# Layer 0 of a two-layer kernel: each product with C directly behind its scan on VectorE

## What is computed

```python
x = hs @ in_proj_w.T                                  # 768 -> 1536 channels
xs = conv3x3_depthwise(x) + conv_b;  xs = xs * sigmoid(xs)
x_dbl = xs_seq @ x_proj_w.T
dt, Bs, Cs = split(x_dbl, [R, R + 4])
delta = softplus(dt @ dt_w.T + dt_b)
dA  = exp(delta[..., None] * A)                       # 4 states per channel
dBu = (delta * u)[..., None] * Bs
states = scan over the pixels:  s = dA * s + dBu
y = einsum('bdln,bln->bdl', states, Cs) + D_param * u
y = layernorm(y over channels);  out = y @ out_proj_w.T
x = x + out
```

## Time and profile before

| | |
|---|---|
| median of 3 runs | 3685.06 us (3684.29 to 3686.72) |
| the profiled execution, its own time | 3683.9 us |
| its span in the profile | 3682.1 us |
| mean granted TensorE clock | 0.967 |
| end of layer 0 in the profile | about 2772 us |
| the slots with scans (17 to 208) | from 263 to about 2715 us |
| page: busy, TensorE / VectorE / ScalarE / GpSimd | 92% / 78% / 64% / 64% of the span |

### The profile page before, as it was taken

One profiled execution on the slowest core, in us unless ns is written; L12 is line 12 of the kernel. 1 busy time (PEld: TensorE's weight loads), 2 busy tenths in 40 slices (PEclk: granted clock), 3 DMA queues, 4 the chain that ended last, 5 costly groups with the idle time before them and its releaser, 6 DMA issues. The chain is left out here.

```text
span 3682.1 us, 39373 instructions
## 1 busy us (share of the span) xinstructions
PE 3382.5 (92%) x10888; PEld 1745.1 (47%) x10888; DVE 2868.8 (78%) x4117; ACT 2345.9 (64%) x4095; POOL 2346.0 (64%) x1557
## 2 busy tenths in 40 slices
PE   5875799999999999999999999998798999999999
PEld 4432234333343344334333343343346877767787
DVE  4469999999999988999999999998754345565532
ACT  1357787887878867877788777887535555443211
POOL 0139898999989978898998989999830001112211
PEclk7897799999999999999999999999899999999999
DMA  7244355555556545555555555555533223356654
GB/s 288 81 144 118 92 137 150 153 148 147 139 149 159 145 130 131 149 142 146 158 144 150 134 147 160 136 160 146 139 87 114 66 83 107 117 191 210 209 199 153
DMA packets 217179, 529.93 MB, mean 144 GB/s; under 512 B 24744, under 2 KB 45928, under 8 KB 214016
## 3 DMA queue, kind: packets, MB, share of 16 engines
q1 hardware_dynamic: 173952, 376.39, 32.5%
q0 software_dynamic: 43008, 151.02, 18.5%
HBM read 346.17 MB, written 80.48 MB: 116 GB/s over the span
## 5 line engine op out<-in xcount | busy, mean ns | idle before, releaser
L575 PE MATMUL p_in<-xn,win_v 128*128 128x512 f32 (+1 forms) x2304 | 1064.3, 611 | 125.4 <-ACT halo L766 83.0
L591 PE MATMUL p_op<-uy,wout_ring 128*128 128x512 f32 x2160 | 987.5, 606 | 39.0 <-DVE x_res L970 38.9
L935 DVE TENSOR_TENSOR_SCAN p_da<-p_da,state,g_ring 128x512 f32<-128x512 f32 x672 | 827.3, 1277 | 107.9 <-ACT p_da L725 70.3
L907 POOL TENSOR_TENSOR g_ring<-du,B_bc 128x2048 f32<-128x2048 f32 x192 | 870.7, 4535 | 16.7 <-DMA B_bc<-bc_scratch 1.8
L956 DVE SCALAR_TENSOR_TENSOR p_cv<-win_v,conv_w,p_cv 128x512 f32<-128x512 f32 x960 | 722.8, 753 | 87.9 <-ACT p_cv L787 67.0
L575 PEld LDWEIGHTS p_in<-xn,win_v 128*128 128x128 f32 x2304 | 440.8, 197 | 705.8 <-issue 705.8
L591 PEld LDWEIGHTS p_op<-uy,wout_ring 128*128 128x128 f32 x2160 | 401.1, 192 | 614.2 <-issue 539.9
L725 ACT ACTIVATE p_da<-delta,A 128x512 f32<-128x512 f32 x768 | 499.4, 682 | 12.5 <-ACT state L730 0.2
L941 DVE TENSOR_TENSOR g_ring<-p_da,C_bc 128x512 f32<-128x512 f32 x768 | 486.9, 675 | 0.0
L1387 PE MATMUL banks<-x_split,w_split 128*128 128x512 f32 x1152 | 458.9, 398 | 11.0 <-DVE x_split L1590 5.5
L1389 PE MATMUL banks<-x_split,w_split 128*128 128x512 f32 x1152 | 450.4, 391 | 0.0
(11 more groups left out here) (220 smaller groups left out, 4070.3 us busy)
## 6 DMA issues: line engine op xcount, KB each, us to landing
g_ring<-g_ring POOLq DMA_DIRECT2D x192, 512.0 KB, 5.6
win_v<-in_win SPq DMA_DIRECT2D x192, 384.0 KB, 3.1
wout_ring<-wout_scratch SPq DMA_DIRECT2D x184, 384.0 KB, 3.8
x_ring<-x_scratch SPq DMA_DIRECT2D x192, 256.0 KB, 2.7
q_scratch<-q_ring POOLq DMA_DIRECT2D x96, 256.0 KB, 2.5
x_split<-q_scratch SPq DMA_DIRECT2D x96, 256.0 KB, 3.4
out<-x_ring POOLq DMA_DIRECT2D x96, 256.0 KB, 3.0
x_res<-in_x SPq DMA_DIRECT2D x90, 256.0 KB, 4.5
```

The source lines that it names most:

```text
L575: last = nc.tensor.matmul(p_in[:, 0:n], WR[:, i % NW, t, :], XN[:, t, off:off + n], start=(t == 0), stop=(t == XT - 1))
L591: last = nc.tensor.matmul(p_op[:], OR[:, e % NO, k - h * HALF, :], ucol(c * K + k), start=(k == 0), stop=(k == K - 1))
L907: nc.gpsimd.tensor_tensor(G[:, i % NG], DU[:].unsqueeze(1).broadcast_to([P, NS, N]), BB[:], ALU.mult).then_inc(s_dbu, 1)
L935: nc.vector.tensor_tensor_scan(bank, bank, G[:, i % NG, n, :], init, ALU.mult, ALU.add)\
```

## The change

In both places of VectorE's list where two scans were followed by two products, each product now stands directly behind its scan. Nothing is added or taken away, no wait is changed, and the lists of the other four engines are the same.

```diff
                     if a is not None:
                         scan(a, 0)
+                        times_c(a, 0)
                         scan(a, 1)
-                        times_c(a, 0)
                         times_c(a, 1)
...
                     if a is not None:
                         scan(a, 2)
+                        times_c(a, 2)
                         scan(a, 3)
-                        times_c(a, 2)
                         times_c(a, 3)
```

## The result

| | before | changed |
|---|---|---|
| median | 3684.68 us (3682.61 to 3686.72, 4 runs) | 3767.12 us (3763.60 to 3770.37, 4 runs) |
| ratio | | 1.0223, 95% interval 1.0210 to 1.0235: slower by 82.4 us |
| profiled execution, its span | 3683.9, 3682.1 us | 3770.37, 3768.6 us |
| mean granted TensorE clock | 0.967 | 0.960 |

The sign and the range of the prediction held; the number, 3739, was 28 us too low. The profiled execution after is 3.3 us above its median, so between the two profiled spans there are 86.5 us to explain.

A forecast was written before the change was run, and what follows sets the result against it. In a regular chunk VectorE sets the pace for 8.5 slots and TensorE for 3.5. Terms +3.4, +20.0, 0, +20.7 and +9.6 sum to +54 us on 3683.9, 3738; with 1.2 for the median, 3739, range 3712 to 3783.

The forecast's parts named there:

- The link: VectorE product directly behind its own scan: 0.09 overlap lost plus 0.035 hole, 0.127 us each, 98 us in all.
- Rival 1: The scan-to-product link is free, the drain being there anyway: nothing added, 3685 us; chance 5%.
- 8.5 slots: Slot 64 to first pair of slot 72, where VectorE sets the pace: 4.3 us more per regular chunk.
- waits at 67 and 72: VectorE's short waits for ScalarE's exponentials before these slots, swallowing about 0.6, leaving 3.7 us a chunk.
- 11.4 regular chunks: Twelve-slot chunks at 3.7 us: 5.4 from 463 to 1290 us (+20.0), six from 1508.7 to 2428.6 (+20.7).
- waits of 2.14 and 2.01: VectorE's waits before scan 2 of slot 63 and scan 0 of slot 64: still there, but smaller.
- Behind the last taps: Closed loop of VectorE and ScalarE, 4.91 us a pair instead of 4.66; its stretch, 2428.6 to 2679.8 us, +9.6.
- Slots 17 to 32: 250 to 463 us: 7.6 us more VectorE work against 4.9 us of waits for exponentials, +3.4 us.
- The cover: In a chunk's other 3.5 slots, the 2.14 us wait before slot 63's scan 2 covers the added 1.8 us.
- Rival 3: Nothing is covered, all 98 us of added VectorE time show: 3783 us; chance 13%.
- Rival 2: Only the one-way path counts, slots 64, 65, 68, 69: 2.0 us a chunk, +32 us, 3717; chance 14%.
- 1290 to 1508.7 us: Around the second image's start: VectorE stood 24.3 us in 13 waits, TensorE 95% busy, so 0 added.

The follow-up runs named there:

- e1_phase_tail: Scan and product alternate only in slots with S % 12 = 1, 2, 3, against the kernel before: 3691.79 us, ratio 1.0018.
- e2_phase_body: Scan and product alternate only in slots from S % 12 = 4 on, against the kernel before: 3757.18 us, ratio 1.0188.
- e11_middle_only: Scan and product alternate only in slots 97 to 111, against the kernel before: one run, 3692.18 us.
- e7_spaced_alternate: The changed kernel's alternation with a tap put between each scan and its product: 3813.30 us, ratio 1.0345 against the kernel before.

## Why the prediction was right or wrong

- **The link.** "Hole of 0.035, overlap of 0.09 lost": right to the nanosecond the trace can show (34 to 36 ns in 538 links). The term that was mis-sized is 0.127 a link, 0.51 a slot: it is 0.15 and 0.60. What was missing is the length: a product behind its own scan takes 692 ns instead of 675, and the second scan of a pair, no longer behind the first, 1283 instead of 1268. I had read the mean of the taps, 753, which mixes 743 and 756; their spread before the change would have shown that a dependent instruction is longer. A link here is always both, one instruction reads what its neighbour wrote and waits for its semaphore; no run parts the two. By 192 slots this is 115 us of VectorE's time instead of 98, and the page's busy time agrees: 86.9 us more, with 768 holes of 0.035 (27 us) that do not count as busy.
- **The rule of the Trainium skill** (VectorE: DVE Perf Modes, "The DRAIN you can't avoid"), that the pipeline empties anyway and a semaphore between two operations costs nothing extra, is not what these runs show: independent neighbours start 0.08 to 0.09 us before the other's end, dependent ones 0.035 behind it and are longer. The prediction took only half of that section of the Trainium skill: it also says that a next operation that is not held starts earlier, and with that the overlap of independent neighbours agrees. Rival 1 falls by all 538 links.
- **What reaches the end.** The count of 8.5 slots was right: 8.5 x 0.60 = 5.1, less 0.3 for the wait before slot 67 and 0.1 at slot 72, gives 4.7; 4.6 was measured at full clock. The prediction let the waits at 67 and 72 swallow 0.6, they gave 0.4: the one at 67 shrank to 0.07 instead of going. Over the 11.4 regular chunks the mis-sized link and these waits are 0.9 x 11.4 = 10 us of the 28 that were missing. The waits of 2.14 and 2.01 are smaller and not gone, as said. Behind the last taps 4.95 a pair came where 4.91 was predicted, and the stretch gave 10.5 for 9.6; it also has 10.3 us more at half clock, so that part of this agreement may be luck. Slots 17 to 32 gave 5.3 for 3.4: 15 slots at 0.09 more are 1.4 of that difference.
- **The cover** in slots 61 to 63 holds: `e1_phase_tail` left the chunk at 153.7. Rival 3 (3783, nothing covered) falls, although the time came out closer to it than to the forecast: it was nearly right by number and wrong by mechanism. Rival 2 (2 us a chunk) falls by `e2_phase_body`.
- **1290 to 1508.7 us, "0".** Right for VectorE's time (`e11_middle_only`), wrong for the sum: +7.2 us. The step that failed was that TensorE's own speed would stay as it was. The prediction had no term for the clock, although its own rows show one stretch at 0.93. In slots 32 to 112 of the changed kernel the clock stood at half for 34 us where the kernel before had no fall; 5.4 chunks at 4.6 explain 25 of the 31.0 us of slots 32 to 97, the rest and the 7.2 lie in stretches with half clock.
- **Elsewhere.** Layer 1 and the end of layer 0 took 5.5 us more, with 13.1 us more at half clock, the start 3.1 less, with 6.8 us less of it, and no instruction was moved in either. I did not test these.

So the 82 us are, in round numbers: 54 predicted, some 13 for the mis-sized link (chunks, slots 17 to 32 and the end), and the rest, about 15, for which more time at half clock is the likely account (64 us more of it in the whole profiled execution). The last figure is what remains, not a measurement, and by it the forecast's range held with something in it that the forecast didn't know of.

## What to carry to other kernels

On an in-order engine, put an independent instruction between two dependent ones, and price a dependent link by both its start and its length (the spread of a group shows the two lengths, its mean hides them). But first find which instruction another engine waits for: moving fillers ahead of that one costs more than the link saves, as `e7_spaced_alternate` did with as little work on VectorE as any kernel here and the longest time. When a change makes a nearly full engine wait longer, expect that its clock may not stay where it was, and say so in the range.

## What the runs showed of the hardware that was not expected

- A product or tap of VectorE on 128 x 512 float32 is longer when it depends on its neighbour ahead: product 692 for 675 ns, tap 756 for 743 to 748. A scan depends on no neighbour here and still has two lengths, 1265 to 1268 ns behind another scan and 1280 to 1286 behind a product or tap. With the hole of 35 ns and the lost overlap of 0.09 us, that is 0.15 us a turned link.
- TensorE's clock fell to half for 3.4 us in the middle of chunks in which TensorE is busy 94%, in six of ten chunks of the changed kernel, against one in the kernel before, which is busy 96%. Before five of these six falls TensorE had stood 2.40 us (2.15 before the other); in the other four chunks it stood as long and kept its clock. Over all runs 33 of 58 chunks with a wait of 1.95 us or more have a fall, and none of the 72 whose longest wait is 1.89 or less. Two more products a chunk only moved the falls, to another wait. One fall cost 0.8 to 1.7 us in a chunk where VectorE sets much of the pace, and half of its length, 3.4 of 6.8 us, in slots 97 to 100 of `e1_phase_tail`.
